# A six-layer windowed-attention stage: inverse-root refinement on GpSimd, the clamp as a rectifier on ScalarE, and new engine orders

## The chip, the cores and the metric

The kernel runs on one core of a Trainium2 chip. The metric is the device time of one launch in microseconds, the median of the runs shown. The engines are TensorE (PE in the profile; its weight loads are PEld), VectorE (DVE), ScalarE (ACT), GpSimd (POOL) and SyncE (SP), whose queue (SPq) issues the DMAs.

## The reference

`x` is 4 x 1024 tokens of 128 features in float32. It is normalised to `xn`; the output is `x + attention(xn) + stack(xn)`. The first is one causal attention with 16 heads of 8. The second is the part that this case is about, six layers on a residual `x`, each of them:

```python
for i in range(6):
    x = attn_layer(shift_tokens(x), Wqkv[i], q_scale[i], k_scale[i], Wo[i]) + x
    x = ffn_layer(shift_tokens(x), ln_g[i], ln_b[i], W1[i], b1[i], W2[i], b2[i]) + x

# attn_layer: 16 heads of 64, q and k normalised, rotated, keys of a band
q = q / maximum(norm(q), 1e-12) * q_scale      # the same for k
q = q * cos * scale + rotate_half(q) * sin * scale
sim = einsum('...ie,...je->...ij', q, k) * 8.0  # own 32 tokens and the 32 before
out = softmax(where(mask, -max, sim)) @ v       # then @ Wo

# ffn_layer: 341 hidden features
xn = (x - mean) / sqrt(var + 1e-5) * g + b
out = (a * gelu(gate)) @ W2 + b2                # a, gate = split(xn @ W1 + b1)
```

`shift_tokens` takes the second half of the features from the token before.

## The kernel before

Four parts run in turn: `prepare` (normalisation), `attention` (the causal attention, up to about 985 us), `windowed` (the six layers) and `finish`. `xa` and `xb` hold the residual with features on partitions; all of it stays in SBUF.

`windowed` goes through the tokens in 16 pairs of tiles of 128 tokens per layer, 96 pairs over six layers, with no barrier between layers. `r` numbers the pair, `u` (0 or 1) the tile of the pair, `i` (or `e`, `par`) the half of the 16 heads. Each step is a small function, called in an order that is written out by hand for each engine in its `body(pair)`. The body runs in a hardware loop, with unrolled rounds before and after it, and mixes steps of four neighbouring pairs (`pair - 3` to `pair`). Engines run in order and wait on semaphores: `chunk(engine, sem, r, u)` waits until the step has been done for that tile, `back=n` for n tiles earlier.

A tile takes this way. ScalarE copies its residual (`build_xs`). TensorE projects q, k and v in halves of 512 columns (`project`, L922) into two PSUM banks `px`, used in turn in the order of `PX_USES`; a projection waits until the bank's use before last has been read, for k by `add_k` on VectorE, for q by `copy_q`, for v by `copy_v`. ScalarE squares q and k (L1121, L1128), VectorE sums them (L1386, L1392). VectorE's `clamp` (L1422) takes the maximum with 1e-24, ScalarE takes the logarithm (`factor_log`, L1153) and the exponential (`factor_seed`, L1159), which gives a rough inverse root; VectorE's `refine` (L1432 to L1436) makes a Newton step of it and leaves the factors in `rn`. Meanwhile k is rotated on VectorE (`rotate_k`, `straight_k`, `add_k`, L1399 to L1414) and q on GpSimd (`rotate_q`, `straight_q`, `add_q`, L1306 to L1320). GpSimd multiplies both by `rn` (`normalise_q`, `normalise_k`, L1328, L1336). TensorE turns them (`turn_k` L932, `turn_q` L942) into two banks `pt`, ScalarE stores them, TensorE computes the scores (`scores`, L953 and L964). VectorE takes the maximum and subtracts it (L1442, L1449), ScalarE the exponential (`exps`), TensorE turns it (`turn_p`) and multiplies by the values (`values`, L992), VectorE scales by the inverse sum (`scale_c`, L1473), TensorE turns that (`turn_c`, L1003) and multiplies by the output weights (`project_out`, L1015), VectorE adds (`add_attention`).

The values come through the window buffers `vw[u]`, one for each tile of a pair. `copy_v` (ScalarE, L1146) writes `v[u]`; SyncE's `windows(r, u)` (L864 to L867) then copies ten overlapping pieces of `v[u]` and `v[1 - u]` to `vw[u]` by DMA. Two waits tie this ring together, one in `windows`, on the values of the pair before, that used the same buffer, and one in `copy_v`, which for `u = 1` wants all ten copies of `windows(r, 0)`, since these read the old `v[1]`:

```python
chunk(sp, valued[i], r, u, back=2 - VALUED_AHEAD)          # windows, VALUED_AHEAD = 2
wait(act, v_windows[1 - u], 16 * WINDOW_DMAS * (r if u == 0 else r + 1))   # copy_v
```

`valued` starts at 2, so the first line asks for the values of tile `u` of pair `r - 1`.

The second half of a layer runs once for each pair: `build_xf`, `ffn_turn` (L1025), `stats` and `aggregate`, `var_log` (L1209) and `var_seed` on ScalarE, `normalise_x` on VectorE (four small steps L1506 to L1512, then the two products L1515), `ffn_back` (L1033), `scale_xn`, and three parts of the hidden features: `ffn_hidden(n)` (L1045, L1046) waits for `gate(n - 1)`, `gelu(n)` (ScalarE, L1229), `gate(n)` (VectorE, L1524); then `ffn_out` (L1053) and `add_ffn`. The gelu and the logarithm need different tables of ScalarE, which are loaded at L1229 and L1231.

Of the kernel before, what the change touches and what calls it, by code (L numbers as in the profile page):

```python
# [9 lines left out]

# [11 lines left out]
P = 128  # L22
# [23 lines left out]
MASKED = -1e30  # L46
RSQRT_MAGIC = float(0x5F3759DF)
# [574 lines left out]
def windowed(nc, t):  # L622
    with ExitStack() as ctx:
# [20 lines left out]
        eps = sb("eps", [P, 1])  # L644
# [11 lines left out]
        ss = sb("ss", [P, 2 * HEADS])  # L656
        ssc = sb("ssc", [P, 2 * HEADS])
# [20 lines left out]
        lt = sb("lt", [P, 2])  # L678
        lr = sb("lr", [P, 2])
# [30 lines left out]
        xf_ready = sem("xf_ready")  # L710
# [6 lines left out]
        with ExitStack() as pre, nc.Block() as block:  # L717
# [44 lines left out]
        def layer_loaded(engine, semaphore, per_layer, r):  # L762
# [5 lines left out]
        PX_USES = (("v", 1, 0, 1), ("q", 0, 0, 1), ("k", 0, 0, 1), ("k", 1, 0, 1), ("q", 1, 0, 1), ("v", 0, 1, 1),  # L768
                    ("v", 1, 1, 1), ("q", 0, 1, 1), ("k", 0, 1, 1), ("k", 1, 1, 1), ("q", 1, 1, 1), ("v", 0, 0, 0))
        PT_USES = (("pt", 1, 0, 2), ("kt", 1, 1, 2), ("pt", 0, 0, 2), ("kt", 0, 1, 2), ("qt", 0, 1, 2), ("ct", 1, 0, 2),  # L770
                    ("qt", 1, 1, 2), ("ct", 0, 0, 2), ("pt", 1, 1, 2), ("pt", 0, 1, 2), ("kt", 1, 0, 1), ("qt", 0, 0, 1),
                    ("kt", 0, 0, 1), ("qt", 1, 0, 1), ("ct", 0, 1, 2), ("ct", 1, 1, 2))
# [136 lines left out]
        def _(pe):  # L909
# [146 lines left out]
            def body(pair):  # L1056
                project(pair - 1, 0, "v", 1)
                ffn_turn(pair - 3)
                project(pair - 1, 0, "q", 0)
                turn_p(pair - 2, 0, 1)  # L1060
                project(pair - 1, 0, "k", 0)
                turn_k(pair - 2, 1, 1)
                values(pair - 2, 0, 1)
                turn_p(pair - 2, 0, 0)
                project(pair - 1, 0, "k", 1)
                turn_k(pair - 2, 1, 0)
                values(pair - 2, 0, 0)
                ffn_back(pair - 3)
                turn_q(pair - 2, 1, 0)
                turn_c(pair - 2, 0, 1)  # L1070
                ffn_hidden(pair - 3, 0)
                turn_q(pair - 2, 1, 1)
                turn_c(pair - 2, 0, 0)
                project(pair - 1, 0, "q", 1)
                project(pair - 1, 1, "v", 0)
                ffn_hidden(pair - 3, 1)
                scores(pair - 2, 1)
                ffn_hidden(pair - 3, 2)
                project(pair - 1, 1, "v", 1)
# [6 lines left out]
                turn_k(pair - 1, 0, 1)  # L1086
                values(pair - 2, 1, 1)
                values(pair - 2, 1, 0)
                turn_q(pair - 1, 0, 0)
                turn_k(pair - 1, 0, 0)  # L1090
# [7 lines left out]
                project(pair, 0, "v", 0)  # L1098

# [5 lines left out]
        def _(act):  # L1105
# [43 lines left out]
            def factor_log(r, u):  # L1149
                if outside(r):  # L1150
                    return
                chunk(act, clamped, r, u)
                nc.scalar.activation(lnv[:], ssc[:], ACT.Ln).then_inc(logged, 1)  # L1153

            def factor_seed(r, u):
# [3 lines left out]
                nc.scalar.activation(seed[:], lnv[:], ACT.Exp, scale=-0.5).then_inc(seeded, 1)  # L1159

# [44 lines left out]
            def var_log(r):  # L1205
# [3 lines left out]
                nc.scalar.activation(lv[:], mv[:, :, 1], ACT.Ln, bias=eps[:]).then_inc(f_logged, 1)  # L1209

            def var_seed(r):
# [3 lines left out]
                nc.scalar.activation(ls[:], lv[:], ACT.Exp, scale=-0.5).then_inc(f_seeded, 1)  # L1215
# [17 lines left out]
            def body(pair):  # L1233
                exps(pair - 2, 0, 1)
                factor_seed(pair - 2, 1)
                build_xf(pair - 3)
                copy_v(pair - 1, 0, 0)
                copy_v(pair - 1, 0, 1)
                exps(pair - 2, 0, 0)
                square_q(pair - 1, 0, 0)  # L1240
                store_p(pair - 2, 0, 1)
                square_k(pair - 1, 0, 0)
                var_log(pair - 3)
                var_seed(pair - 3)
                copy_q(pair - 1, 0, 0)
                store_kt(pair - 2, 1, 1)
                store_p(pair - 2, 0, 0)
                square_k(pair - 1, 0, 1)
                store_kt(pair - 2, 1, 0)
                build_xs(pair - 1, 1)  # L1250
                scale_xn(pair - 3)
                store_qt(pair - 2, 1, 0)
                store_c(pair - 2, 0, 1)
                gelu(pair - 3, 0)
                square_q(pair - 1, 0, 1)
                store_qt(pair - 2, 1, 1)
# [124 lines left out]
        def _(dve):  # L1381
# [331 lines left out]
```

## Time and profile before

| | before |
|---|---|
| median of 3 runs | 4577.74 us (4577.34 to 4584.95) |
| profiled execution | 4593.52 us, its span 4591.7 us |
| busy in the span | PE 4043.8, PEld 2700.9, DVE 3732.5, ACT 2817.7, POOL 2502.8 us |
| instructions | 176379 |
| mean granted clock of TensorE | 0.942 |
| DMA | 250.44 MB, 55 GB/s in the mean |

Busy times are sums of instructions; an engine that isn't busy waits for a semaphore or has an empty queue. In the traces L-numbers are lines of this kernel. Times in the time lines count from the start of the span. A granted clock of 1.00 is TensorE's 2.4 GHz, 0.50 is 1.2 GHz.

### The profile page before, as it was taken

Reading aid. Unit: us, or ns where it says so; the run is one execution under the profiler, and the core shown is the slowest. Engines: PE = TensorE matmul, PEld = TensorE weight load, DVE = VectorE, ACT = ScalarE, POOL = GpSimd, SP = SyncE. Lnnn points to the kernel's source line nnn. Section 1 sums busy time; section 2 is a strip of 40 time slices with the busy share of each in tenths; the row PEclk is TensorE's granted clock in tenths of the full one; section 3 lists DMA queues with packets and bytes.
Section 4 is the critical chain, followed back from the end, with each engine's and each line's share of the span. In section 5 each row is a group of like instructions: output and inputs, shape, how many; then the busy total and the mean of one; then the engine's idle time right before and its main releaser. Section 6 shows DMA issues by size and latency. Waiting matters only on the chain. (4 is left out here: it accounts for less than half of the span.)

```text
span 4591.7 us, 176379 instructions
## 1 busy us (share of the span) xinstructions
PE 4043.8 (88%) x67601; PEld 2700.9 (59%) x67840; DVE 3732.5 (81%) x7589; ACT 2817.7 (61%) x5554; POOL 2502.8 (55%) x2355
## 2 busy tenths in 40 slices
PE   4588778778999999999999999999999999999997
PEld 2233333346666666666666666666666666666665
DVE  7676566468888888888888888888888888888886
ACT  4154444456666666666666666666666666666664
POOL 4000000056666666666666666666666666666663
PEclk7698898989999999999999999999999999999998
DMA  2322121032222222222222223222232222222221
GB/s 78 47 27 32 22 29 15 11 94 56 56 55 55 66 68 56 57 60 60 74 55 55 55 55 79 59 57 57 55 79 55 55 55 57 69 57 55 55 55 47
DMA packets 176308, 250.44 MB, mean 55 GB/s; under 512 B 46918, under 2 KB 65988, under 8 KB 175300
## 3 DMA queue, kind: packets, MB, share of 16 engines
q1 hardware_dynamic: 176196, 248.94, 22.5%
q8 instruction: 71, 1.16, 0.1%
q14 instruction: 41, 0.34, 0.0%
HBM read 39.08 MB, written 8.39 MB: 10 GB/s over the span
## 5 line engine op out<-in xcount | busy, mean ns | idle before, releaser
L922 PE MATMUL w_px<-w_wqkv,w_xs 128*128 (+1 forms) x2304 | 1164.5, 608 | 61.0 <-DVE w_kr L1414 32.6
L1306 POOL TENSOR_TENSOR w_qr<-w_raw,w_tc 128x512 f32<-128x512 f32 x384 | 486.2, 1277 | 512.9 <-ACT w_raw L1136 333.6
L1313 POOL TENSOR_TENSOR w_qrot<-w_raw,w_tc 128x512 f32<-128x512 f32 x384 | 481.8, 1277 | 451.4 <-ACT w_raw L1136 451.4
L505 ACT ACTIVATE a_probs<-a_wide 128x256 f32<-128x256 f32 (+7 forms) x512 | 309.4, 649 | 401.2 <-PE a_wide L419 397.9
L922 PEld LDWEIGHTS w_px<-w_wqkv,w_xs 128*128 128x128 f32 x2304 | 380.9, 192 | 267.4 <-issue 187.0
L1320 POOL TENSOR_TENSOR w_qr<-w_qr,w_qrot 128x512 f32<-128x512 f32 x384 | 489.6, 1275 | 0.0
L1328 POOL TENSOR_TENSOR w_qr<-w_qr,w_rn 128x512 f32<-128x512 f32 x384 | 402.1, 1047 | 146.1 <-DVE w_rn L1436 138.5
L548 DVE TENSOR_REDUCE a_row_max<-a_ring 128x1 f32<-128x512 f32 (+3 forms) x512 | 298.7, 591 | 210.3 <-PE a_ring L394 116.9
L1336 POOL TENSOR_TENSOR w_kr<-w_kr,w_rn 128x512 f32<-128x512 f32 x384 | 397.3, 1045 | 65.0 <-DVE w_rn L1436 65.0
L1015 PEld LDWEIGHTS w_pw<-w_ot,w_wo 128*128 128x128 f32 x3072 | 368.2, 193 | 61.1 <-issue 50.9
L1015 PE MATMUL w_pw<-w_ot,w_wo 128*128 128x128 f32 x3072 | 387.3, 280 | 5.6 <-issue 4.4
L531 POOL COPY a_v_pad<-a_v_all 128x256 f32 (+1 forms) x16 | 6.4, 402 | 688.5 <-PE a_out L433 688.4
L1182 ACT ACTIVATE w_p<-w_p 128x512 f32<-128x512 f32 x384 | 240.9, 630 | 200.5 <-DVE w_p L1449 200.5
L1524 DVE SCALAR_TENSOR_TENSOR w_hid<-w_pf,w_b,w_gl 128x256 f32<-128x256 f32 (+1 forms) x288 | 138.4, 481 | 276.5 <-ACT w_gl L1229 276.5
L391 PE MATMUL a_ring<-a_k_stack,a_q_stack 96*128 96x512 bf16 (+3 forms) x768 | 262.2, 351 | 108.6 <-DVE a_row_max L548 44.5
L1128 ACT ACTIVATE w_qsq<-w_px 128x512 f32<-128x512 f32 x384 | 227.8, 593 | 210.2 <-PE w_px L922 210.0
L964 PEld LDWEIGHTS w_sc<-w_kt,w_qt 64*32 64x32 f32 x24576 | 263.7, 105 | 88.4 <-issue 86.4
L992 PE MATMUL w_sc<-w_vw,w_pts 64*32 64x64 f32 x24576 | 310.1, 225 | 2.1 <-issue 2.1
L1442 DVE TENSOR_REDUCE w_mx<-w_sc 128x8 f32<-128x512 f32 x384 | 262.3, 683 | 55.6 <-PE w_sc L964 55.6
L964 PE MATMUL w_sc<-w_kt,w_qt 64*32 64x64 f32 x24576 | 297.2, 225 | 4.5 <-issue 4.5
L992 PEld LDWEIGHTS w_sc<-w_vw,w_pts 64*32 64x32 f32 x24576 | 263.3, 105 | 50.8 <-issue 50.8
L1399 DVE TENSOR_TENSOR w_turn<-w_px,w_tc 128x512 f32<-128x512 f32 x384 | 263.6, 686 | 34.3 <-ACT w_ksq L1121 30.9
(154 smaller groups left out, 9558.8 us busy)
## 6 DMA issues: line engine op xcount, KB each, us to landing
w_vw<-w_v SPq DMA_DIRECT2D x1152, 128.0 KB, 2.3
w_vw<-w_v SPq DMA_DIRECT2D x768, 64.0 KB, 2.0
a_q_stack<-q_parts SPq DMA_DIRECT2D x144, 64.0 KB
a_k_stack<-k_parts SPq DMA_DIRECT2D x144, 64.0 KB
w_wqkv<-in_L_ffn_Wqkv SPq DMA_DIRECT2D x6, 1536.0 KB, 6.1
q_parts<-ap_parts SPq DMA_DIRECT2D x8, 384.0 KB, 2.5
k_parts<-ap_parts SPq DMA_DIRECT2D x8, 384.0 KB, 2.5
w_wo<-in_L_ffn_Wo SPq DMA_DIRECT2D x24, 128.0 KB, 2.8
```

Of the source, the lines that this page charges most:

```text
L505: nc.scalar.activation(probs[kc % 2][:, hh, 0:width], wide_bank[w % 2][:, 0:width], ACT.Exp).then_inc(exp_done, 1)
L548: nc.vector.tensor_reduce(into, bank_at(hg, n)[:, 0:width], AX.X, ALU.max).then_inc(r_done, 1)
L922: nc.tensor.matmul(px[bank_of(PX_USES, what, i, u)][:], xs[u][:], rhs, start=True, stop=True).then_inc(done, 1)
L964: mm = nc.tensor.matmul(sc[e][rows, WIN * j:WIN * (j + 1)], qt[u][d, j, rows], kt[u][d, j, BAND * w:BAND * w + WIN], start=False, stop=Tru ...
L992: mm = nc.tensor.matmul(sc[par][rows, at:at + HD], pts[e][keys, n, rows], vw[u][keys, w, at:at + HD], start=True, stop=True, skip_group_ch ...
L1015: mm = nc.tensor.matmul(pw[:, 0:P], wo[:, n, :], ot[n // 4][:, (n % 4) * P:(n % 4 + 1) * P], start=(n == 0), stop=(n == 7))
L1306: nc.gpsimd.tensor_tensor(by_head(qr[i][:]), by_head(raw[i][:]), wide(table(u, Q_COS)), ALU.mult).then_inc(q_straight[i], 1)
L1313: nc.gpsimd.tensor_tensor(halves(qrot[i][:]), swapped(raw[i][:]), split_table(u, Q_SIN), ALU.mult).then_inc(q_rotated[i], 1)
L1320: nc.gpsimd.tensor_tensor(qr[i][:], qr[i][:], qrot[i][:], ALU.add).then_inc(q_added[i], 1)
L1328: nc.gpsimd.tensor_tensor(by_head(qr[i][:]), by_head(qr[i][:]), factor, ALU.mult).then_inc(q_normal[i], 1)
L1336: nc.gpsimd.tensor_tensor(by_head(kr[i][:]), by_head(kr[i][:]), factor, ALU.mult).then_inc(k_normal[i], 1)
L1399: nc.vector.tensor_tensor(halves(turn[i][:]), swapped(px[bank_of(PX_USES, "k", i, u)][:]), split_table(u, K_SIN), ALU.mult).then_inc(k_tur ...
```

## The change

1. The clamp moves from VectorE to ScalarE, as `over = relu(ss - 1e-24)`; the logarithm takes 1e-24 back as its bias, `log(over + 1e-24)`.
2. `refine` moves from VectorE (three operations) to GpSimd (five: the clamped sum `ssc = over + tiny`, the square of the seed, the product, `3 - step`, the product with the seed), with a wait of GpSimd on itself between dependent ones.
3. The four small steps of `normalise_x` move to GpSimd as `refine_x` (five operations of two columns). The exponential of `var_seed` gets a bias.
4. `sum_k` and `sum_q` wait for the clamp of the tile before.
5. The order of every engine's `body` is new, and the body now begins at `project_out(pair - 2, 0)`, so that its second half works on the next pair; `PX_USES` and `PT_USES` follow. SyncE's program isn't changed.

```diff
+            def clamp(r, u):
+                for i in range(2):
+                    chunk(act, k_summed[i], r, u)
+                    chunk(act, q_summed[i], r, u)
+                chunk(act, factors_ready, r, u, back=1)
+                nc.scalar.activation(over[:], ss[:], ACT.Relu, bias=less_tiny[:]).then_inc(clamped, 1)
...
-                nc.scalar.activation(lnv[:], ssc[:], ACT.Ln).then_inc(logged, 1)
+                nc.scalar.activation(lnv[:], over[:], ACT.Ln, bias=tiny[:, 0:1]).then_inc(logged, 1)
...
+            def refine(r, u):
+                pool.sem_clear(chain)
+                chunk(pool, seeded, r, u)
+                nc.gpsimd.tensor_tensor(ssc[:], over[:], tiny[:], ALU.add).then_inc(chain, 1)
+                nc.gpsimd.tensor_tensor(step[:], seed[:], seed[:], ALU.mult).then_inc(chain, 1)
+                pool.wait_ge(chain, 2)
+                nc.gpsimd.tensor_tensor(step[:], step[:], ssc[:], ALU.mult).then_inc(chain, 1)
+                pool.wait_ge(chain, 3)
+                nc.gpsimd.tensor_tensor(step[:], three[:], step[:], ALU.subtract).then_inc(chain, 1)
+                pool.wait_ge(chain, 4)
+                nc.gpsimd.tensor_tensor(rn[u][:], step[:], seed[:], ALU.mult).then_inc(factors_ready, 1)
+            def refine_x(r):
...
+                wait(pool, f_seeded, r + 1)
+                nc.gpsimd.tensor_tensor(le[:], mv[:, :, 1], eps[:], ALU.add).then_inc(x_chain, 1)
```

The new orders, from `values(.., 0, 0)` to the hidden products (in the new numbering of pairs; what ran before there, in the same numbering, is on the left):

```text
TensorE before                 TensorE after
values(pair-1, 0, 0)           values(pair-1, 0, 0)
ffn_back(pair-2)               ffn_back(pair-2)
turn_q(pair-1, 1, 0)           turn_q(pair-1, 1, 0)
turn_c(pair-1, 0, 1)           turn_c(pair-1, 0, 1)
ffn_hidden(pair-2, 0)          ffn_hidden(pair-2, 0)
turn_q(pair-1, 1, 1)           turn_c(pair-1, 0, 0)
turn_c(pair-1, 0, 0)           project(pair, 1, "v", 0)
project(pair, 0, "q", 1)       turn_q(pair-1, 1, 1)
project(pair, 1, "v", 0)       project(pair, 0, "q", 1)
ffn_hidden(pair-2, 1)          ffn_hidden(pair-2, 1)
scores(pair-1, 1)              scores(pair-1, 1)
ffn_hidden(pair-2, 2)          ffn_hidden(pair-2, 2)

ScalarE before                 ScalarE after
scale_xn(pair-2)               scale_xn(pair-2)
store_qt(pair-1, 1, 0)         store_qt(pair-1, 1, 0)
store_c(pair-1, 0, 1)          store_c(pair-1, 0, 1)
gelu(pair-2, 0)                gelu(pair-2, 0)
square_q(pair, 0, 1)           store_qt(pair-1, 1, 1)
store_qt(pair-1, 1, 1)         copy_v(pair, 1, 0)
copy_q(pair, 0, 1)             square_q(pair, 0, 1)
gelu(pair-2, 1)                gelu(pair-2, 1)
copy_v(pair, 1, 0)             copy_q(pair, 0, 1)
store_c(pair-1, 0, 0)          store_c(pair-1, 0, 0)
gelu(pair-2, 2)                clamp(pair, 0)
```

Elsewhere: on ScalarE `factor_seed` now directly follows `factor_log` for tile 0, and for tile 1 comes before `exps(.., 0, 1)`; `square_k(.., 1, 0)` comes before `square_q(.., 1, 0)`; a `store_p(.., 0, 1)` comes before `square_q(.., 0, 0)`. On VectorE `stats` and `aggregate` come one sum earlier. GpSimd's part:

```diff
                 rotate_q(pair - 1, 0, 1)
                 tables(pair - 1, 1)
+                refine(pair - 1, 0)
+                add_q(pair - 1, 0, 1)
+                normalise_k(pair - 1, 0, 1)
+                normalise_k(pair - 1, 0, 0)
                 normalise_q(pair - 1, 0, 0)
-                normalise_k(pair - 1, 0, 1)
...
+                refine(pair - 1, 1)
+                straight_q(pair - 1, 1, 1)
+                tables(pair, 0)
+                normalise_k(pair - 1, 1, 1)
+                normalise_k(pair - 1, 1, 0)
+                refine_x(pair - 2)
+                normalise_q(pair - 1, 1, 0)
```

## Rows read from the trace of the kernel before

**Rows 1.** Windows: length, busy us of PE, PEld, DVE, ACT, POOL, then clock, DMA share, GB/s.

```profile
1000.00:2000.00 1000.00, 927.79 (x17390) 657.13 (x17441) 864.73 (x1723) 673.70 (x1356) 672.49 (x637) 0.97 0.23 59
```

**Rows 2.** Waits, 1000 to 4500 us: waiting line, releaser, us in total, times, longest.

```profile
PE w_pf L1033 <- DVE w_xnt L1515: 141.9, 93, 1.8
...
PE w_px L922 <- DVE w_kr L1414: 30.5, 86, 0.4
...
PE w_pt L1003 <- DVE w_cx L1473: 29.5, 92, 0.3
...
ACT w_v L1146 <- DMA w_vw<-w_v: 5.8, 4, 2.5
```

**Rows 3.** Time line of TensorE, `ffn_back`: start, us, what, [wait before, releaser].

```profile
1007.46 0.49 PE L1033 MATMUL w_pf<-ident,w_xnt 128*128 128x128 f32 x2 [1.77 <-DVE w_xnt L1515]
...
2511.52 0.44 PE L1033 MATMUL w_pf<-ident,w_xnt 128*128 128x128 f32 x2 [1.49 <-DVE w_xnt L1515]
...
2549.80 0.44 PE L1033 MATMUL w_pf<-ident,w_xnt 128*128 128x128 f32 x2 [1.51 <-DVE w_xnt L1515]
...
2586.39 0.44 PE L1033 MATMUL w_pf<-ident,w_xnt 128*128 128x128 f32 x2 [1.51 <-DVE w_xnt L1515]
...
4539.20 0.44 PE L1033 MATMUL w_pf<-ident,w_xnt 128*128 128x128 f32 x2 [0.40 <-DVE w_xnt L1515]
```

**Rows 4.** Windows of TensorE alone behind the first of these waits.

```profile
2513.00:2516.00 3.00, 3.00 (x13) 0.50 0.63 163
```

**Rows 5.** Time line of TensorE: `values(0, 0)` ends, hidden product 2 starts.

```profile
2547.43 0.86 PE L992 MATMUL w_sc<-w_vw,w_pts 64*32 64x64 f32 x64
...
2557.74 0.66 PE L1045 MATMUL w_pf<-w_xnf,w_w 128*85 128x256 f32 x2
```

**Rows 6.** Time line of all engines and SyncE's queue (SPq), the same stretch.

```profile
2548.36 0.54 SPq L864 DMA_DIRECT2D w_vw<-w_v  x1
...
2552.76 1.87 SPq L867 DMA_DIRECT2D w_vw<-w_v  x3
...
2554.29 0.60 ACT L1128 ACTIVATE w_qsq<-w_px 128x512 f32<-128x512 f32 x1 [0.23 <-PE w_px L922]
...
2556.01 0.47 ACT L1229 ACTIVATE w_gl<-w_pf,w_b 128x256 f32<-128x256 f32 x1 [0.16 <-PE w_pf L1046]
...
2556.43 0.59 ACT L1146 COPY w_v<-w_px 128x512 f32<-128x512 f32 x1
2556.52 0.48 DVE L1524 SCALAR_TENSOR_TENSOR w_hid<-w_pf,w_b,w_gl 128x256 f32<-128x256 f32 x1 [1.35 <-ACT w_gl L1229]
```

**Rows 7.** DMA issues of 2548 to 2556 us: count, KB each, us to landing.

```profile
w_vw<-w_v SPq DMA_DIRECT2D x6, 128.0 KB, 2.3
```

**Rows 8.** Groups by line, 1000 to 4500 us, VectorE: count, busy us, mean ns.

```profile
L1422 DVE TENSOR_SCALAR w_ssc<-w_ss 128x32 f32<-128x32 f32 x186 | 133.5, 718 | 19.0 <-DVE w_ss L1386 19.0
...
L1434 DVE TENSOR_TENSOR w_step<-w_step,w_ssc 128x32 f32<-128x32 f32 x186 | 35.8, 192 | 6.4
```

**Rows 9.** The same view, GpSimd and one of ScalarE.

```profile
L1306 POOL TENSOR_TENSOR w_qr<-w_raw,w_tc 128x512 f32<-128x512 f32 x372 | 471.0, 1278 | 492.8 <-ACT w_raw L1136 315.5 <-PE w_pt L942 177.4
...
L1336 POOL TENSOR_TENSOR w_kr<-w_kr,w_rn 128x512 f32<-128x512 f32 x374 | 387.0, 1045 | 63.8 <-DVE w_rn L1436 63.8
...
L1297 POOL TENSOR_TENSOR w_tc<-w_rope_tab,w_scales 128x256 f32 x184 | 135.0, 734 | 0.0
...
L1348 POOL TENSOR_TENSOR w_kt<-w_kt,w_keep 128x256 f32<-128x256 f32 x93 | 57.1, 614 | 0.0
...
L1209 ACT ACTIVATE w_lv<-w_mv,w_eps 128x2 f32<-128x2 f32 x94 | 26.9, 286 | 0.1
```

**Rows 10.** Time line, 2558 to 2566 us: last `gelu`, logarithm, turned `kr`.

```profile
2558.88 0.47 ACT L1229 ACTIVATE w_gl<-w_pf,w_b 85x256 f32<-85x256 f32 x1 [1.37 <-PE w_pf L1046]
...
2560.66 0.23 ACT L1153 ACTIVATE w_lnv<-w_ssc 128x32 f32<-128x32 f32 x1
...
2565.30 0.60 PE L932 MATMUL w_pt<-ident,w_kr 128*128 128x128 f32 x4
```

More of the change, by code:

```diff
@@ L656, in windowed @@
         ss = sb("ss", [P, 2 * HEADS])
+        over = sb("over", [P, 2 * HEADS])
         ssc = sb("ssc", [P, 2 * HEADS])
@@ L739, in _ @@
                 nc.vector.memset(eps[:], 1e-5)
+                nc.vector.memset(tiny[:], 1e-24)
+                nc.vector.memset(less_tiny[:], -1e-24)
+                nc.vector.memset(three[:], 3.0)
+                nc.vector.memset(near[:], math.log(NEWTON_AT))
+                nc.vector.memset(top[:], 1.5 / NEWTON_AT)
                 nc.vector.memset(keep[:, 0:1], 0.0)
@@ L1278, in body @@
                 square_q(pair - 1, 1, 1)
+                store_c(pair - 2, 1, 0)
+                store_c(pair - 2, 1, 1)
                 copy_q(pair - 1, 1, 1)
-                store_c(pair - 2, 1, 1)
-                store_c(pair - 2, 1, 0)
+                clamp(pair - 1, 1)
                 factor_log(pair - 1, 1)
+                build_xs(pair, 1)
+                factor_seed(pair - 1, 1)
+                exps(pair - 1, 0, 1)
+                build_xf(pair - 2)
+                copy_v(pair, 0, 0)
+                copy_v(pair, 0, 1)
+                exps(pair - 1, 0, 0)
+                store_p(pair - 1, 0, 1)
+                square_q(pair, 0, 0)
+                var_log(pair - 2)
+                square_k(pair, 0, 0)
+                var_seed(pair - 2)
+                copy_q(pair, 0, 0)
+                store_kt(pair - 1, 1, 1)
+                store_p(pair - 1, 0, 0)
+                square_k(pair, 0, 1)
+                store_kt(pair - 1, 1, 0)
+                scale_xn(pair - 2)
+                store_qt(pair - 1, 1, 0)
+                store_c(pair - 1, 0, 1)
+                gelu(pair - 2, 0)
+                store_qt(pair - 1, 1, 1)
+                copy_v(pair, 1, 0)
+                square_q(pair, 0, 1)
+                gelu(pair - 2, 1)
+                copy_q(pair, 0, 1)
+                store_c(pair - 1, 0, 0)
+                clamp(pair, 0)
             nc.scalar.preload_act_table_set("natural_log_exp_and_others")
@@ L1537, in body @@
             def body(pair):
-                add_k(pair - 2, 1, 1)
-                clamp(pair - 2, 1)
-                max_scores(pair - 2, 0, 1)
-                shift_scores(pair - 2, 0, 1)
-                max_scores(pair - 2, 0, 0)
-                add_attention(pair - 3, 1)
-                shift_scores(pair - 2, 0, 0)
-                refine(pair - 2, 1)
-                sum_p(pair - 2, 0, 1)
-                stats(pair - 3)
-                sum_p(pair - 2, 0, 0)
-                sum_q(pair - 1, 0, 0)
@@ L1588, in body @@
                 sum_q(pair - 1, 1, 1)
+                add_k(pair - 1, 1, 1)
+                max_scores(pair - 1, 0, 1)
+                shift_scores(pair - 1, 0, 1)
+                add_attention(pair - 2, 1)
+                max_scores(pair - 1, 0, 0)
+                shift_scores(pair - 1, 0, 0)
+                stats(pair - 2)
+                sum_p(pair - 1, 0, 1)
+                aggregate(pair - 2)
+                sum_p(pair - 1, 0, 0)
+                sum_q(pair, 0, 0)
+                invert(pair - 1, 0)
+                rotate_k(pair, 0, 0)
+                straight_k(pair, 0, 0)
+                normalise_x(pair - 2)
+                add_k(pair, 0, 0)
+                scale_c(pair - 1, 0, 1)
+                scale_c(pair - 1, 0, 0)
+                rotate_k(pair, 0, 1)
+                straight_k(pair, 0, 1)
+                add_k(pair, 0, 1)
+                gate(pair - 2, 0)
+                sum_k(pair, 0, 0)
+                sum_k(pair, 0, 1)
+                gate(pair - 2, 1)
+                sum_q(pair, 0, 1)
+                max_scores(pair - 1, 1, 1)
+                max_scores(pair - 1, 1, 0)
             dve.sem_inc(xa_ready, PAIRS)
```

235 lines of the change are left out of this document (89 added, 146 removed).

## The prediction

> **What bounds the kernel now.** I read the windows by stage first, then the waits, then the time line of TensorE, and last the four queues side by side. The windows show all four engines fairly full in the six-layer stage, TensorE fullest at 928 us of 1000, VectorE at 865, ScalarE and GpSimd near 673 [rows 1]. The time line gives the rhythm: `ffn_back` (L1033) starts once for each pair, first at 1007.46 and last at 4539.20 with 94 periods between, so a pair takes 37.57 us in the mean [rows 3]. Two neighbouring periods are not alike: 2511.52 to 2549.80 is 38.28 us and 2549.80 to 2586.39 is 36.59 us [rows 3]. The 1.69 us between them are the clock. Soon after the first of these starts three microseconds run at a granted clock of 0.50 (1.2 GHz instead of 2.4) [rows 4], and the stretch follows on TensorE's wait of 1.49 us at `ffn_back`. If the two sorts of period are mixed to give 37.57, (37.57 - 36.59) / 1.69 = 0.58 of the pairs pay for a slow stretch.
>
> TensorE waits in few places [rows 2]: for the normalised activations at L1033 (141.9 us over 93 pairs, 1.53 each), for `kr` before a projection (30.5, 0.33 each), for `cx` before its transpose (29.5, 0.32 each). All else is its own work. So the pair is TensorE's work plus waits plus clock, and an edit is worth what it takes from or adds to these three.
>
> One more queue matters, which looks harmless in the waits: ScalarE waited for the window copies by DMA only 4 times (5.8 us) [rows 2]. The time line shows how near that is. `values(pair, 0, 0)` ends at 2547.43 + 0.86 = 2548.29 [rows 5]. SyncE's first window copy of the next tile starts at 2548.36, right behind, because `vw` has one buffer per half. Ten issues follow, the last of them the third of a group that ends at 2554.63, so it starts at about 2554.04 [rows 6]; it lands 2.3 us later [rows 7], at 2556.34. That is 8.05 us after the values. `copy_v(r, 1, 0)` must wait for all ten, as it overwrites the `v[1]` that they read; in this fast pair it starts at 2556.43, just behind a `gelu` that ended at 2556.48 [rows 6] (neighbours overlap by some 0.05). In the present order the wait costs nothing because the copy stands after `gelu(.., 1)`.
>
> **The change, part by part.** I call the end of `values(.., 0, 0)` V.
>
> *VectorE loses work.* Both clamps, both three-step `refine` chains and the four small operations of `normalise_x` go. The clamp alone is 133.5 us over 93 pairs, 1.44 each, for 32 columns [rows 8]. VectorE isn't what the pair waits for, except through L1033. Cost or gain by itself: nothing; the cover is TensorE's own work. What it does is to bring `xnt` forward.
>
> *L1033.* The variance chain now goes ScalarE (`var_log`, `square_k`, `var_seed`), five operations on GpSimd, then VectorE. The `add_attention` and `stats` before it move up by two operations, and GpSimd reaches `refine_x` after two `normalise_k` instead of in the thick of its additions. I reckon `xnt` about 1 us before V, against 1.5 us after it now. So this wait of 1.51 us goes. The wait for `kr` goes too (0.33), since `add_k(.., 1, 0)` now has `square_k` ahead of `square_q`, and the wait of `cx` stays in part, as its VectorE operation can't start before V.
>
> *GpSimd gains fifteen small operations.* No row has one so small. From below: a product of 512 columns is 1.278, of 256 columns 0.734 [rows 9], so 2.1 ns a column on a base of 0.19; 32 columns give 0.26, two columns 0.19. From above: 0.614, the shortest product of GpSimd in the trace (256 columns) [rows 9]. I take the line, and 0.1 us more for each wait of the chain on itself, since these widths lie at its base: `refine` 5 x 0.26 + 3 x 0.1 = 1.6, `refine_x` 1.3, together 4.5 us a pair on an engine with 0.67 x 37.57 = 25 us of work. Hidden, if the one tight place holds: from hidden product 2 (2557.74) `gelu` starts 1.14 later, the logarithm 2.92 later, and TensorE wants the turned `kr` (L932) 7.56 later [rows 5, 10]. In the new order log, seed (0.3 each with what lies between), `refine` 1.6, an addition 1.28 and `normalise_k` 1.05 [rows 9] follow: 2.95 + 0.6 + 1.6 + 1.28 + 1.05 = 7.5. It just fits. Each 0.1 us more per small operation costs 0.5 us a pair there.
>
> The Trainium skill (GPSIMD Engine Reference, section 4.1, Engine selection) speaks against this move: ordinary elementwise work belongs on VectorE, which is about twice as fast. No row here has a small GpSimd operation to test it. By it, twice VectorE's 0.192 [rows 8] makes 0.38 for each, `refine` 2.2 instead of 1.6, and some 0.5 us a pair more than my sum, 4669 us.
>
> *ScalarE gains two clamps and two bias operands.* An activation of 32 columns is 0.23 [rows 10], one of two columns with a bias tile 0.286 [rows 9]; so at most 0.35 each for the clamps and 0.1 for each bias, 0.9 us a pair on an engine with 25 us of work in 37.57. Below nothing is excluded, for nothing is taken away. Hidden: it waits for others more than 10 us a pair.
>
> *The order of ScalarE.* Here is the price. `copy_v(pair, 1, 0)` moves from behind `gelu(.., 1)` to before it, and before `square_q(pair, 0, 1)`. SyncE's program is untouched, so its ten issues still start at V and land at V + 8.05. The copy can't start sooner. Behind it in the queue stand the square, `gelu(.., 1)`, `copy_q`, `store_c`; behind `gelu` the gate on VectorE, behind that hidden product 2 on TensorE. Durations in turn 0.59, 0.60, 0.47 and 0.48 [rows 6], less 0.1 for overlap: hidden product 2 at V + 8.05 + 2.04 = V + 10.1. Now it starts at 2557.74, V + 9.45 [rows 5]. TensorE's work from V to there is 9.45 - 1.51 - 0.32 = 7.6 us, so it reaches the product with some 2.4 us to wait. The 1.51 us that L1033 gives back are lost again here, with 0.65 more.
>
> *The rest of the period.* From hidden product 2 to the next V the same instructions run, in a slightly other order, 36.59 - 9.45 = 27.14 us, less 0.33 for `kr` and about 0.2 for an `xf` that is earlier: 26.6. A period at full clock is then 10.1 + 26.6 = 36.7, against 36.59.
>
> *The clock.* A wait of 1.5 us is followed by a slow stretch in 0.58 of the pairs [rows 3, 4]. The new one is 2.4 us. Bounds: no pair (0) and every pair (1.69). I take a share of 0.8, above the present one as the wait is longer: 1.34. Period 36.7 + 1.34 = 38.04, 0.47 above 37.57, times 94 periods is 44 us. Start, attention stage and end are untouched; the turned loop body starts at another point of the same round, for which I take nothing, within a few microseconds. The profiled execution took 4593.52 (span 4591.7), 0.3% over the median; I add the difference to the median: 4577.74 + 44 = 4622.
>
> **The rivals.**
> *The window wait doesn't bind* (copies land sooner than I read, or other work fills it). Then all of L1033 and the slow stretches go: 36.59 - 1.51 - 0.33 - 0.2 - 0.2 = 34.35, 3.22 less in each of 94 periods, 303 us: 4275. For it: VectorE's relief is real, and the order leaves no other wait that I found. Against it: the 8.05 us rest on the issue times. It decides for "faster" once the copy can start at V + 5.5 or sooner.
> *It binds, but the clock stays up.* 36.7, 0.87 less: 82 us less, 4496. This is the one that ends on the other side with my mechanism intact; it takes a share of slow pairs under about 0.45 to be faster by more than 0.2%. Against it: a shorter wait already brings the clock down in more than half of the pairs.
> *The share stays at 0.58.* 37.68, 10 us more: 4588, no change to within a few microseconds.
> *GpSimd is dearer.* At 0.41 for each small operation `refine` takes 0.75 more: 70 us over my forecast, 4692; at the upper bound of 0.61 it takes 1.75 more, 4786. For it: three waits on itself in a row. Against it: the line through the rows.
> *Further table loads*, if Relu lies in another set than the one loaded: two of 1.28 us (the gap between `gelu` and log holds one [rows 10]), 240 us. Unlikely.
>
> **How the numbers follow.** My forecast (share 0.6 to 1, 4590 to 4654) 0.50; share as now 0.10; clock stays up 0.14; window wait doesn't bind 0.10; GpSimd dearer 0.13; tables and others 0.03. The range 4490 to 4700 leaves out the free case, the dear half of GpSimd's and the tables, 0.18. My forecast's own range is 4588 to 4660. Slower by over 0.2% (9 us, what a measurement of this kernel can tell): 0.50 + 0.13 + 0.03 and a little of the third, 0.68; faster 0.14 + 0.10 less a little, 0.23; within, 0.09.
>
> **What the profile after would show.** L1033's wait on TensorE near nothing; ScalarE waiting for the window copies at `copy_v` some 3 us in every pair; TensorE waiting some 2.4 us for the gate before hidden product 2; periods of about 36.7 and 38.4; small GpSimd operations of 0.2 to 0.3. I am wrong if the copy starts much before V + 8, if the clock stays at 1.00 through that wait, or if L932 waits for `normalise_k`.

## The result, and the profile after

The changed kernel takes 4607.17 us (median of 4 runs, 4598.51 to 4610.52), the kernel before 4579.33 on the same chip (4 runs, 4577.34 to 4584.95). The ratio is 1.0056, with a 95% interval of 1.0038 to 1.0073: slower by 28 us, by more than the 0.2% that count as a difference here. The forecast was slower, 4622.

The profiled execution of after took 4598.51 us, the shortest of its four; that of before took 4593.52, longer than any of the four it is compared by. So the two traces lie only 5 us apart where the medians lie 28. The traces show which waits went and which came; the other 23 us are spread between executions of one kernel. For before the granted clock goes with that spread: on one chip of the experiments its executions reach from 4574.35 us at a mean granted clock of 0.946 to 4593.05 at 0.942, and the profiled one had 0.942.

| | after |
|---|---|
| span of the profiled execution | 4596.7 us |
| busy in the span | PE 4027.7, PEld 2704.2, DVE 3285.3, ACT 2912.0, POOL 2811.8 us |
| instructions | 177076 |
| mean granted clock of TensorE | 0.928 |

The windows by stage of after, columns as in [rows 1]:

```profile
1000.00:2000.00 1000.00, 920.71 (x17327) 655.28 (x17379) 741.95 (x1404) 699.25 (x1406) 757.82 (x1037) 0.96 0.23 59
```

VectorE is down by 123 us in 1000, GpSimd up by 85, ScalarE up by 26. TensorE, the fullest, is busy for 7 us less and granted a little less clock: almost nothing of VectorE's relief has arrived.

The waits of after (compare [rows 2]):

```profile
ACT w_v L1161 <- DMA w_vw<-w_v: 343.2, 94, 8.0
...
PE w_pf L1060 <- DVE w_hid L1556: 254.2, 93, 6.9
```

The three waits of TensorE in [rows 2] are gone. One has taken their place, before the hidden products (L1060 was L1045): 2.73 us in each of 93 pairs, more than the 1.53 + 0.33 + 0.32 that went. And ScalarE, which waited 4 times for the window copies, now waits 94 times, 3.65 each. The time line of one pair, TensorE, ScalarE, VectorE and SyncE's queue (compare [rows 5, 6]):

```profile
2509.68 0.86 PE L1007 MATMUL w_sc<-w_vw,w_pts 64*32 64x64 f32 x64
...
2510.47 0.44 PE L1048 MATMUL w_pf<-ident,w_xnt 128*128 128x128 f32 x2
...
2510.61 0.54 SPq L879 DMA_DIRECT2D w_vw<-w_v  x1
...
2513.91 0.48 ACT L1255 ACTIVATE w_gl<-w_pf,w_b 128x256 f32<-128x256 f32 x1
...
2515.01 1.87 SPq L882 DMA_DIRECT2D w_vw<-w_v  x3
...
2518.73 0.58 ACT L1161 COPY w_v<-w_px 128x512 f32<-128x512 f32 x1 [3.53 <-DMA w_vw<-w_v]
...
2519.70 0.48 ACT L1255 ACTIVATE w_gl<-w_pf,w_b 128x256 f32<-128x256 f32 x1
...
2520.21 0.48 DVE L1556 SCALAR_TENSOR_TENSOR w_hid<-w_pf,w_b,w_gl 128x256 f32<-128x256 f32 x1 [4.12 <-ACT w_gl L1255]
...
2520.74 1.02 PE L1060 MATMUL w_pf<-w_xnf,w_w 128*85 128x256 f32 x2 [2.58 <-DVE w_hid L1556]
```

Read it from the end. Hidden product 2 at 2520.74 waited 2.58 for the gate (L1556), the gate for the `gelu` at 2519.70, and this stood in ScalarE's queue behind `copy_v` at 2518.73, which waited 3.53 for the copies by DMA; the last of these was issued in the group that begins at 2515.01, the first at 2510.61, just behind `values(.., 0, 0)`, which ended at 2509.68 + 0.86 = 2510.54. All of the chain hangs on that end, V. `ffn_back` at 2510.47 waits for nothing.

The time line of TensorE, `ffn_back` (L1048), and one hidden product at the start of a layer (compare [rows 3]):

```profile
1002.61 0.44 PE L1048 MATMUL w_pf<-ident,w_xnt 128*128 128x128 f32 x2
...
1602.17 0.44 PE L1048 MATMUL w_pf<-ident,w_xnt 128*128 128x128 f32 x2
...
1616.89 1.15 PE L1060 MATMUL w_pf<-w_xnf,w_w 128*85 128x256 f32 x2 [6.93 <-DVE w_hid L1556]
...
1643.90 0.33 PE L1048 MATMUL w_pf<-ident,w_xnt 128*128 128x128 f32 x1
...
2548.02 0.44 PE L1048 MATMUL w_pf<-ident,w_xnt 128*128 128x128 f32 x2
...
4542.79 0.44 PE L1048 MATMUL w_pf<-ident,w_xnt 128*128 128x128 f32 x2
```

From first to last, 94 periods: 37.66 us each, against 37.57 before. One period in the middle (2510.47 to 2548.02) is 37.55. In before two sorts alternated, 36.6 and 38.3; here nearly all are 37.3 to 37.6, except four of 41.2 to 41.7, one at each of four starts of a layer, such as 1602.17 to 1643.90, 41.7 us: there TensorE waits 6.93 for the gate.

Windows of TensorE alone around the new wait (compare [rows 4]): length, busy us, clock, DMA share, GB/s.

```profile
2519.00:2520.00 1.00, 0.00 (x0) 1.00 0.00 0
2520.00:2521.00 1.00, 0.26 (x1) 0.96 0.00 0
2521.00:2524.00 3.00, 3.00 (x6) 0.50 0.00 0
2524.00:2525.00 1.00, 1.00 (x8) 0.84 0.00 0
```

TensorE idles through 2519 to 2520, starts the product at 2520.74, and then works at a granted clock of 0.50, its 1.2 GHz, up to 2524 and a little beyond (0.84 in the next microsecond).

Groups of GpSimd and ScalarE in after (compare [rows 9]):

```profile
L1185 ACT ACTIVATE w_over<-w_ss,w_less_tiny 128x32 f32<-128x32 f32 x186 | 59.8, 321 | 31.6 <-DVE w_ss L1455 31.6
...
L1375 POOL TENSOR_TENSOR w_step<-w_step,w_ssc 128x32 f32<-128x32 f32 x186 | 46.8, 252 | 14.6
...
L1387 POOL TENSOR_TENSOR w_le<-w_mv,w_eps 128x2 f32<-128x2 f32 x92 | 17.9, 194 | 111.8 <-ACT w_ls L1241 111.8
```

### The profile page after: what moved, and what is told of

It is laid out like the page before. It is cut to its first block and busy times, and to the rows that moved or that the text cites. A ratio compares the mean times of both kernels' runs of the same rounds, so it can differ in the third digit from the quotient of the medians.

```text
span 4596.7 us, 177076 instructions
## 1 busy us (share of the span) xinstructions
PE 4027.7 (88%) x67601; PEld 2704.2 (59%) x67840; DVE 3285.3 (71%) x6442; ACT 2912.0 (63%) x5746; POOL 2811.8 (61%) x3795
## 5 line engine op out<-in xcount | busy, mean ns | idle before, releaser
L937 PE MATMUL w_px<-w_wqkv,w_xs 128*128 (+1 forms) x2304 | 1215.2, 631 | 26.4 <-DMA w_scales<-in_L_ffn_k_scale 20.2
L937 PEld LDWEIGHTS w_px<-w_wqkv,w_xs 128*128 128x128 f32 x2304 | 404.8, 203 | 194.5 <-issue 173.1
L1556 DVE SCALAR_TENSOR_TENSOR w_hid<-w_pf,w_b,w_gl 128x256 f32<-128x256 f32 (+1 forms) x288 | 138.1, 480 | 462.4 <-ACT w_gl L1255 462.4
L1030 PEld LDWEIGHTS w_pw<-w_ot,w_wo 128*128 128x128 f32 x3072 | 402.4, 206 | 105.0 <-issue 95.2
L1161 ACT COPY w_v<-w_px 128x512 f32<-128x512 f32 x384 | 214.8, 584 | 368.2 <-DMA w_vw<-w_v 355.8
L1060 PE MATMUL w_pf<-w_xnf,w_w 128*128 128x256 f32 (+1 forms) x576 | 205.1, 443 | 261.0 <-DVE w_hid L1556 260.2
L1030 PE MATMUL w_pw<-w_ot,w_wo 128*128 128x128 f32 x3072 | 408.0, 289 | 1.2 <-ACT w_ot L1222 0.8
L1136 ACT ACTIVATE w_ksq<-w_px 128x512 f32<-128x512 f32 x384 | 229.6, 598 | 164.2 <-PE w_px L937 156.8
L1193 ACT COPY w_kt<-w_pt 128x512 f32<-128x512 f32 x384 | 224.4, 584 | 156.1 <-PE w_pt L947 144.8
L1524 DVE TENSOR_TENSOR xb<-w_pw,xa 64x128 f32 (+1 forms) x384 | 111.1, 289 | 288.7 <-PE w_pw L1030 286.0
```

The source lines that it names most:

```text
L937: nc.tensor.matmul(px[bank_of(PX_USES, what, i, u)][:], xs[u][:], rhs, start=True, stop=True).then_inc(done, 1)
L1030: mm = nc.tensor.matmul(pw[:, 0:P], wo[:, n, :], ot[n // 4][:, (n % 4) * P:(n % 4 + 1) * P], start=(n == 0), stop=(n == 7))
```

## The experiments

My theory: the copy to `v[1]` is held by ten window copies that start at V, and in the new order of ScalarE the `gelu` of hidden part 1 stands behind it. Rivals: GpSimd's small chains are the new bound; the orders as such cost the time; the clock does. A period is the time from one `ffn_back` to the next. All ratios are to the kernel before on the same chip; its medians were 4577 to 4588 on the chips used, so differences in microseconds between kernels are good to some 5 us.

**e1: after, with a shorter wait.** Only two of the ten window copies read the other tile's `v`. They go first and on a semaphore of their own, and `copy_v` waits for those two alone.

```diff
-                wait(act, v_windows[1 - u], 16 * WINDOW_DMAS * (r if u == 0 else r + 1))
+                wait(act, v_tails[1 - u], 16 * TAIL_DMAS * (r if u == 0 else r + 1))
```

> The kernel after, with the window wait shortened: the two copies of windows(r, u) that read the other tile's v are issued first and counted on a semaphore of their own, and copy_v waits for these two alone. Theory (the window wait holds hidden product 2): copy_v(pair, 1, 0) can start about 0.1 + 0.6 + 2.0 + 0.6 = 3.3 us behind the values, before ScalarE reaches it (4.7), so its wait goes, TensorE's wait of 2.6 us before hidden product 2 goes, and with it the slow stretch of 1.7 us in each pair. Period 37.5 - 2.6 - 1.7 = 33.2, with new small waits 33.5 to 34.5, time 4200 to 4310. Rival (the wait is a symptom, gelu and gate would come late anyway, or GpSimd's refine holds the next turned kr): TensorE waits elsewhere by 1 us or more and the time stays over 4400.

Measured 4204.63 us, ratio 0.9174 (0.9159 to 0.919). A window of one stage first (columns as in [rows 1]), then the time line of one pair in it:

```profile
2000.00:3000.00 1000.00, 991.20 (x19528) 711.09 (x19586) 838.88 (x1584) 788.00 (x1580) 852.44 (x1164) 1.00 0.26 68
```

```profile
2510.52 0.86 PE L1013 MATMUL w_sc<-w_vw,w_pts 64*32 64x64 f32 x64
...
2515.94 0.59 ACT L1167 COPY w_v<-w_px 128x512 f32<-128x512 f32 x1
...
2518.94 0.66 PE L1066 MATMUL w_pf<-w_xnf,w_w 128*85 128x256 f32 x2
```

V is 2511.38; the copy (L1167) starts 4.56 behind it without a wait, hidden product 2 at V + 7.56 without a wait, and TensorE is busy 991 of 1000 us at a granted clock of 1.00. So the wait that I named carries not 28 us but 402 (4607.17 to 4204.63): the rest of the change is worth some 375 us, and this one wait ate it all.

**e2: after, with the copy moved back** behind `store_c(pair - 1, 0, 0)`, the wait left at ten copies.

```diff
-                copy_v(pair, 1, 0)
                 square_q(pair, 0, 1)
...
                 store_c(pair - 1, 0, 0)
+                copy_v(pair, 1, 0)
```

> The kernel after, with copy_v(pair, 1, 0) moved on ScalarE from before square_q(pair, 0, 1) to behind store_c(pair-1, 0, 0); the transfers are as they are. Theory: the copy still starts about 8.1 us behind the values, but gelu 1 no longer stands behind it; hidden product 2 comes about 7.6 us behind the values. The copy may now push the clamp and the last gelu by some tenths. Period 34 to 35.5, time 4260 to 4380. Rival: the copy delays the clamp, the last gelu and with it refine on GpSimd, so that TensorE waits 1 to 2 us for the turned kr; period 36 to 37 and a slow stretch in part of the pairs, time 4450 to 4600.

Measured 4277.03, ratio 0.9337 (0.932 to 0.9354). The same cause from the other side: with the copies as they were, the place of one `copy_v` in ScalarE's queue is worth 330 us. ScalarE still waits for the DMA, 1.1 us a pair (100.4 us over 93), with no `gelu` behind it that is in a hurry; e1, where it doesn't wait, is 72 us shorter.

**e3: before, with the copy moved forward** to behind `gelu(pair - 3, 0)`, ahead of `square_q(pair - 1, 0, 1)`.

> The kernel before, with this one step moved: copy_v(pair-1, 1, 0) on ScalarE goes from behind gelu 1 to behind gelu 0, ahead of square_q(pair-1, 0, 1), as in the kernel after. Theory: hidden product 2 goes from 9.45 to 10.1 us behind the values, TensorE waits for ffn_back and again before hidden product 2 (0.7 us more in pairs at full clock). Period 37.2 at full clock, slow stretches in at least the share of now: 38.2 in the mean, time 4600 to 4700. Rival (the copy's place doesn't matter in this order, and the loss of the kernel after lies elsewhere, as in GpSimd's refine): no change, 4570 to 4590.

Measured 4712.18, ratio 1.0279 (1.0261 to 1.0296): 127 us slower, just above what I expected, and by another way. Waits of TensorE, and two rows of the time line:

```profile
PE w_sc L964 <- ACT w_qt L1175: 145.0, 90, 4.6
PE w_pf L1033 <- DVE w_xnt L1515: 136.4, 90, 1.6
```

```profile
2540.24 0.58 ACT L1146 COPY w_v<-w_px 128x512 f32<-128x512 f32 x1 [2.35 <-DMA w_vw<-w_v]
...
2542.09 1.47 PE L964 MATMUL w_sc<-w_kt,w_qt 64*32 64x64 f32 x128 [1.85 <-ACT w_qt L1175]
```

In the order of before, `store_qt(.., 1, 1)` stands behind the square, so the late copy holds up the scores (L964), 1.6 us a pair, ahead of the hidden product. And L1033 keeps its wait. Both waits are paid here; in after L1033's is gone, which is why after loses 28 us and e3 loses 127.

**e4: before, with the shorter wait of e1.**

> The kernel before, with the same shortened window wait as in the first kernel of this set. Theory: here the copy stands behind gelu 1 and the wait didn't hold it in ordinary pairs, so there is nothing to win but at the starts of four layers (waits of 0.6 to 2.5 us): 4570 to 4580, within 0.2% of before. Rival (issuing the window copies in another order helps by itself, or delays the values): over 0.5% away.

Measured 4581.04 (10 runs), ratio 0.9989 (0.9974 to 1.0003): nothing. In before the wait isn't in the way, and cutting it alone isn't worth a thing.

**e5 and e9: after, the wait filled.** Products of the identity with itself, whose result nothing reads, stand ahead of `ffn_hidden(pair - 2, 2)`, so that TensorE is busy while it would wait: 16 in e5, 10 in e9. This prices the clock by itself.

```diff
+                for _ in range(16):   # e9: 10
+                    nc.tensor.matmul(pw[:, 2 * P:3 * P], t.ident[:], t.ident[:], start=True, stop=True)
                 ffn_hidden(pair - 2, 2)
```

> The kernel after, with 16 products of the identity with itself put on TensorE between scores(pair-1, 1) and hidden product 2, into columns of the pw bank that nothing reads. They do nothing for the result; at 0.11 us each they fill about 1.8 us of the wait of 2.6 us. Theory (the wait itself brings the clock down): the slow stretch behind it goes in all or nearly all pairs, the granted clock is 1.00 throughout, period 37.5 - 1.7 = 35.8, time 4607 - 94 x 1.7 = 4447. Rival (the low clock comes from elsewhere, or the filler doesn't count): period as it is or longer, 4600 to 4620.

> The kernel after with 10 products of the identity with itself on TensorE between scores(pair-1, 1) and hidden product 2 (they do nothing for the result). The first filler of 16 took 3.7 us, 0.23 each, more than the wait of 2.6; 10 take 2.3 and fit. Theory (the wait brings the clock down, 1.7 us in each pair): granted clock 1.00, hidden product 2 at 10.2 us behind the values as in the kernel after, period 35.8, time 4440 to 4455. Rival (the filler's own time is part of the result, the clock's share is smaller): over 4500.

Measured 4543.12, ratio 0.99 (0.9883 to 0.9916), and 4523.0, ratio 0.9875 (0.9858 to 0.9892). TensorE's time line of e5, then of e9:

```profile
2530.13 3.84 PE L1075 MATMUL w_pw<-ident 128*128 128x128 f32 x32
2533.80 0.59 PE L1060 MATMUL w_pf<-w_xnf,w_w 128*85 128x256 f32 x2
```

```profile
2518.79 0.86 PE L1007 MATMUL w_sc<-w_vw,w_pts 64*32 64x64 f32 x64
...
2527.20 2.50 PE L1075 MATMUL w_pw<-ident 128*128 128x128 f32 x20
2529.87 0.66 PE L1060 MATMUL w_pf<-w_xnf,w_w 128*85 128x256 f32 x2 [0.17 <-DVE w_hid L1563]
...
2534.91 1.12 PE L937 MATMUL w_px<-w_wqkv,w_xs 128*128 x2 [0.45 <-ACT w_v L1168]
```

The filler's rows count two matmuls for each product. e5's took 3.7 us, longer than the wait it fills, so it missed its expectation and says only that the granted clock stays at 1.00 when the wait is filled. e9's took 2.5, the product still waited 0.17 for the gate, at V + 10.22, and the granted clock was 1.00 in all ordinary pairs; from 1000 to 4000 us its trace has only three stretches at 0.50, at starts of layers. The ordinary period is 36.55, so the slow stretch costs 37.55 - 36.55 = 1.0 us a pair, not the 1.69 that my expectation of 4440 to 4455 had for it; that expectation failed, and its rival's time (over 4500) came. The last row says why: at full clock TensorE reaches the projection (L937) too early and waits 0.45 for another `copy_v`. Over the whole stage this wait, which in after came 3 times, comes in 90 pairs:

```profile
PE w_px L937 <- ACT w_v L1168: 39.6, 90, 0.5
```

ScalarE's queue is itself late by what the DMA held it, and part of the slow stretch lay over that lateness: 1.69 less 0.44 here and 0.17 at the product is 1.08.

**e6 and e7: e1 with VectorE's work given back.** e6 takes the four steps of `normalise_x` back to VectorE; e7 also both clamps and both `refine`. What is left of the change in e7 is the orders.

> The kernel after with the shortened window wait (first set, 4205 us), and the variance chain back on VectorE: the five operations of refine_x go from GpSimd, the four of normalise_x come back. Theory: VectorE's chain takes 2.6 us where it meets GpSimd's long products, against 1.3 on GpSimd; the other half of the earlier xnt is due to the order. L1033's wait comes back in part, 0 to 0.8 us, period 33.3 to 34.1, time 4205 to 4290. Rival (the place of this chain is what removed the wait of 1.5 us): wait 1.5 us, slow stretches in half of the pairs, 4400 or more.

> As the one before, and the clamp and refine are back on VectorE too (the clamp behind the last sum, refine where the kernel before has it in VectorE's order), so that only the new orders and the shortened window wait are left of the change. Theory: VectorE has 33 us of work in a pair; with a period near 33.5 it becomes the engine that sets the pace, 34.5 to 36, time 4310 to 4460. Rival (the orders alone are the gain and VectorE's relief is worth nothing): within 0.5% of 4205.

Measured 4438.56, ratio 0.9676 (0.9658 to 0.9694), and 4583.4 (10 runs), ratio 0.9994 (0.9982 to 1.0006). TensorE's wait at `ffn_back` in e6, and the time line of the four small steps there with GpSimd beside them:

```profile
PE w_pf L1054 <- DVE w_xnt L1560: 146.8, 94, 3.1
```

```profile
2530.68 0.20 DVE L1551 TENSOR_TENSOR w_lt<-w_ls 128x2 f32<-128x2 f32 x1
...
2530.83 1.04 POOL L1362 TENSOR_TENSOR w_qr<-w_qr,w_rn 128x512 f32<-128x512 f32 x1
2530.92 0.97 DVE L1553 SCALAR_TENSOR_TENSOR w_lt<-w_mv,w_lt 128x2 f32<-128x2 f32 x1
...
2531.83 1.27 POOL L1347 TENSOR_TENSOR w_qrot<-w_raw,w_tc 128x512 f32<-128x512 f32 x1
...
2531.92 1.20 DVE L1555 TENSOR_SCALAR w_lt<-w_lt 128x2 f32<-128x2 f32 x1
...
2533.16 0.16 DVE L1557 TENSOR_TENSOR w_lr<-w_lt,w_ls 128x2 f32<-128x2 f32 x1
```

The same wait in e7, and its window of a stage:

```profile
PE w_pf L1054 <- DVE w_xnt L1576: 221.5, 94, 2.5
```

```profile
1000.00:2000.00 1000.00, 930.19 (x17296) 676.28 (x17350) 881.79 (x1720) 681.02 (x1350) 671.47 (x635) 0.95 0.23 59
```

e1 to e6 to e7: 4205, 4439, 4583. Taken back in this sequence, the four small steps are worth 234 us, the clamps and refinements another 145, and the orders without them nothing, with the short wait. Both expectations failed. Of e6 I had expected a wait of 0 to 0.8 us at `ffn_back` and 4205 to 4290; it is 1.56 (146.8 over 94), as its rival said, and slow stretches stand behind it in 28 of 94 pairs. I had expected 4310 to 4460 of e7: the orders were to be worth something by themselves, and aren't.

With everything on VectorE, `xnt` is late by 2.36 us (221.5 over 94), all ordinary periods are 37.5 or 37.6, and the mean clock of the stage is 0.95.

The time line of e6 shows what makes the chain dear: L1553 and L1555, each on two columns, take 0.97 and 1.20 us, and each ends within 0.03 us of GpSimd's product of 512 columns beside it; their neighbours take 0.16 and 0.20. It is no accident of this pair: of the 95 instances of each in e6 from 1000 to 4500 us, 93 of L1553 and 92 of L1555 take over 0.35 us, and every one of these ends within 0.05 us of the end of a GpSimd instruction. The kernel before has it too, at the second and fourth step:

```profile
2546.46 1.18 DVE L1508 SCALAR_TENSOR_TENSOR w_lt<-w_mv,w_lt 128x2 f32<-128x2 f32 x1
...
2548.02 0.96 DVE L1512 TENSOR_TENSOR w_lr<-w_lt,w_ls 128x2 f32<-128x2 f32 x1
```

The four steps take 2.7 us there, from 2546.28 to 2548.98, and `xnt` comes 1.51 us too late for `ffn_back`. At the 0.15 and 0.31 us of the other two steps, these two would be shorter by 1.5 to 1.8 us together (an estimate), about the whole wait.

**e8: e1 with five more waited small operations in each `refine`** (the first sum, repeated), to see where GpSimd's chain begins to bind.

> The kernel after with the shortened window wait (4205 us), and five more small operations in each refine on GpSimd, each waited for (about 0.33 us each, 1.65 in all), which only repeat the first. Theory (the chain from the last gelu over refine and normalise_k to the turned kr just fits, as the wait of 0.18 us at L952 in the first set says): TensorE waits 1.5 us more in each pair, period 34.9, time 4350, more if the clock falls. Rival (there is slack, the 0.18 us are the ordinary lead of a weight load): under 4230.

Measured 4374.99, ratio 0.9533 (0.9517 to 0.9549). TensorE's wait, and two windows right behind one instance of it, at 2505.99:

```profile
PE w_pt L952 <- POOL w_kr L1370: 144.8, 94, 1.7
```

```profile
2506.00:2510.00 4.00, 4.00 (x144) 1.00 0.07 16
2510.00:2514.00 4.00, 3.95 (x143) 1.00 0.61 156
```

The wait stands where the prediction had it, at L932 of before (L952 here), 1.54 us in the mean. The five additional operations begin at 2500.46 in the same stretch, and the first of the old ones starts 1.81 us behind:

```profile
2502.27 0.25 POOL L1382 TENSOR_TENSOR w_ssc<-w_over,w_tiny 128x32 f32<-128x32 f32 x1 [0.23 <-POOL w_ssc L1379]
```

The period goes from 33.5 to 35.3 in the mean, by the same 1.8: all of the longer chain is paid, no slack was left, and "it just fits" was right. The clock stayed at 1.00 behind a wait of 1.5 us.

**e10: before, with 6 filler products ahead of `ffn_back`**, the clock's price there.

> The kernel before with 6 such products (1.4 us) put ahead of ffn_back, where TensorE waits 1.5 us. Theory: the periods of 38.3 us go, all are 36.6, time 4580 less 94 x 0.97 = 4489. Rival (the clock falls for another reason, as the DMAs that run at that time): both sorts of period stay, 4570 to 4590.

Measured 4495.33, ratio 0.9821 (0.9804 to 0.9838); nearly all periods 36.6, clock 1.00. By the periods of the two traces the slow stretches of before cost 37.57 - 36.6 = 0.97 us a pair, as 0.58 times 1.69 said; by the medians it is 82 us, 0.88 a pair.

**e11 and e12: before, with `refine_x` on GpSimd and nothing else** (behind `normalise_q(pair - 2, 1, 0)`, with the bias of `var_seed` that belongs to it); e12 adds the shorter wait.

```diff
                 normalise_q(pair - 2, 1, 0)
+                refine_x(pair - 3)
```

> The kernel before with one part of the change alone: the variance chain on GpSimd (refine_x, behind normalise_q(pair-2, 1, 0)), all else, orders too, as it was. Theory (of the whole change this part removes the wait at L1033, and copy_v stands behind gelu 1 here): wait at L1033 0 to 0.4 us instead of 1.5, no slow stretches, period 35.1 to 35.8, the copy now waits for the windows by about 1.5 us, which delays store_c and the last gelu a little; time 4345 to 4415. Rival (without the new orders VectorE or the window wait takes it back): 4500 or more.

> As the one before, with the shortened window wait as well. Theory: the copy's wait goes, the last gelu and store_c come on time: 10 to 60 us less than the one before. It stays above 4205, as VectorE keeps clamp and refine and TensorE's order isn't the new one. Rival: no difference to the one before.

Measured 4370.63, ratio 0.9547 (0.9531 to 0.9564), and 4360.81, ratio 0.9523 (0.9507 to 0.9539). Waits of e11 on TensorE and on ScalarE, and its windows from 1000 to 4000 us:

```profile
PE w_pf L1041 <- DVE w_xnt L1531: 5.9, 3, 3.9
```

```profile
ACT w_v L1154 <- DMA w_vw<-w_v: 162.5, 94, 4.3
```

```profile
1000.00:4000.00 3000.00, 2899.27 (x55775) 2041.65 (x55943) 2558.04 (x5190) 2160.44 (x4339) 2224.86 (x2466) 1.00 0.25 64
```

A small part of the change alone gives 207 us: L1033's wait (L1041 here) is gone from all but 3 pairs, and with it the slow stretches, clock 1.00. ScalarE waits 1.7 us a pair for the copies here too, and it is nearly harmless, because in the old order nothing urgent stands behind: e12, without that wait, is only 10 us shorter.

## Why the prediction was right, and where its sizes were off

**The direction and the mechanism** were right, each at its place. The copy was forecast at V + 8.05 and started at 2518.73, V + 8.19; hidden product 2 at V + 10.1, measured V + 10.20; TensorE's wait 2.4, measured 2.58 there and 2.73 in the mean. e1, e2 and e3 show that it is this wait and this place in the queue: shortened or moved, the time falls by 402 or 330 us; put into before, it rises by 127. But the sign rests on a small difference of two large amounts, some 375 us gained and 402 lost, so a modest error in either could have turned it.

**L1033's wait** went, as forecast, and those for `kr` and `cx` with it, of which I had kept the last in part. The two sorts of period that I forecast, 36.7 and 38.4, didn't appear: nearly all are one sort.

**GpSimd's small operations** were forecast at 0.26 and 0.19 and measured at 0.252 and 0.194. The rule of the Trainium skill (GPSIMD Engine Reference, section 4.1, Engine selection), twice VectorE's time, would have made 0.38: the trace shows 0.252 against 0.192 [rows 8], 1.3 times, and the measurement decides. e8 shows that TensorE would have paid for the difference.

**ScalarE's additions** were at most 0.35 a clamp; measured 0.321, hidden.

**The clock** is the term of the sum that was mis-sized. I took a share of 0.8 of the pairs at 1.69 us each, 1.34. The share is all of them, but each costs 1.0 (e9). 1.69 was read from before, where TensorE alone sets the pace; behind the new wait ScalarE is as late, and hides part of it. The rest of the period came to 26.35 (e9: 36.55 less 10.2, with the 0.44 at L937 in it) instead of 26.6. Together 10.2 + 26.35 + 1.0 = 37.55, against 38.04 forecast. The long waits at the starts of layers, which I hadn't counted, add 0.16 in the mean, which gives 37.7.

By the traces the mean period grew by 37.66 - 37.57 = 0.09 us, times 94 some 9 us, and by the medians the time grew by 28; forecast were 44. That the medians come nearer to the forecast than the traces is partly luck. The share of 0.58 was read from an execution of before that is 14 us over the median; at 1.69 us a slow stretch these are some 8 of the 94 pairs (an estimate). The forecast took the slow stretches of that long execution for those of the median, so it counted too little for the change there and too much in the price of 1.69, and the two errors partly cancelled.

**"VectorE's relief by itself: nothing"** was wrong in weight, though no wrong number came of it here. All three waits of TensorE in [rows 2] are on VectorE, the largest at L1033, and that one brought the clock down as well. Its removal alone is worth 207 us (e11); the wait (142 us, [rows 2]) and the clock (82 us, e10) make 224 together, so most of both arrived. The "free case" of 4275 was too dear as well: e1 is at 4205, 33.5 us a pair. The last 70 us I can't split between the clamps, the refinements and TensorE's order: e7 shows only that the order without the relief gives nothing.

**Why VectorE's small steps were so dear** no step of my sum asked, and by the estimate above it is where the wait of 1.5 us at L1033 came from. The rows of e6 and of before show two of them lasting until GpSimd's product ends. The Trainium skill (SBUF — State Buffer, section "Who interferes with whom") says that some VectorE operations are blocked for the whole of a GpSimd instruction; by that rule the trace agrees, and the clamp's 718 ns for 32 columns [rows 8] is another such case: 87 of its 186 instances take over 0.35 us, and each of these ends within 0.05 us of the end of a GpSimd instruction.

The best version is e1, the change with the two copies that matter waited for alone: 4204.63 us, 8.3% under before.

## What to carry to other kernels

Before an instruction is moved forward in an engine's queue, look up what it waits for and what is queued behind it: a wait that never shows in the profile may be hidden only by the work ahead of it, and e2 and e1 show 330 to 402 us hanging on one copy. Where a semaphore counts a batch of DMAs and the reader needs two of them, give these two a semaphore of their own and issue them first; this pays where the reader is in the way (e1), and gave nothing where it wasn't (e4). Small VectorE steps on the path to TensorE are worth looking up beside GpSimd's long products: here two of them were longer, by about the largest wait of TensorE, than the same steps beside them. And a change that moves the time by 0.6% may hold a gain of 8% and a loss of 9%: compare which waits went and which came, not the total.

## What the runs showed of the hardware

The length of a wait of TensorE didn't decide by itself whether the granted clock fell behind it. Counted in the traces, over 94 pairs each: behind a wait of 1.5 us at `ffn_back` a stretch at 0.50 came in 54 pairs of before and 51 of e4; behind 1.56 us at the same place in 28 of e6, with 26 pairs in a row that had none; in e3, with a second wait of 1.6 us later in the pair, in 36. Behind waits of 2.36 (e7) and 2.73 us (after) it came in 94 and in 91. And in e8 a wait of 1.54 us at L952 was followed by a granted clock of 1.00 in all but 4. The work ahead differs between e8 and before (full-width products ahead of L952, the 64 x 32 products of `values` ahead of `ffn_back`), but e6 has the wait and the work ahead of before and half its share. So neither explains it alone, and what decides stays open.

Filler products that nobody reads keep the clock up, and where nothing else is late they pay: 6 of them took before from 4578 to 4495 (e10).

A slow stretch costs less where another engine's queue is late too: 1.0 us in after, against 1.69 in before.
